# A decoder layer with a mixture of experts on one core: the experts' first layer as seven block products of half-sized matrices in place of eight, and the cross-attention's normalisation moved from VectorE to GpSimd

## The reference

```python
x = layernorm(x + self_attention(x))            # 16 heads of 16, rotary positions
x = layernorm(x + cross_attention(x, context))  # masked keys, biases
# mixture of 8 experts, 2 per token, capacity 1280 tokens each
h = gelu(einsum("ecd,edh->ech", buf, w1) + b1, approximate=False)   # 256 -> 1024
out = einsum("ech,ehd->ecd", h, w2) + b2                            # 1024 -> 256
x = layernorm(x + sum over the token's two experts of gate * out)
```

## Time and profile before

| | |
|---|---|
| median of 3 runs | 2143.32 us (2142.54 to 2143.4) |
| the profiled execution, its own time | 2142.94 us |
| its span, first to last instruction | 2140.8 us |
| attentions, busy: PE, DVE, POOL | 1469.0, 1160.5, 689.4 of 1548.4 us |
| experts, busy: PE, DVE, ACT, POOL | 573.3, 141.3, 155.1, 150.8 of 592.4 us |
| mean granted clock of TensorE | 0.98 |

### The profile page before, as it was taken

How to read it: one execution, slowest core, us unless ns; L and a number is a source line. 1 busy time by engine, 2 the same in 40 slices (tenths; PEclk the granted TensorE clock), 3 DMA queues, 4 the chain that set the end, 5 groups by cost and what they waited for, 6 DMA issues and landing times. The chain is left out here.

```text
span 2140.8 us, 55059 instructions
## 1 busy us (share of the span) xinstructions
PE 2042.3 (95%) x21891; PEld 1516.0 (71%) x21891; DVE 1301.8 (61%) x2740; ACT 989.1 (46%) x1515; POOL 840.1 (39%) x1134
## 2 busy tenths in 40 slices
PE   7899999999999999999999999988699999999996
PEld 4667777777776777777777767766478787878785
DVE  5678778788778787787887787865211111111146
ACT  1455555555555555555555555544231212121233
POOL 3333454544444444545445444432412121212144
PEclk8899999999999999999999999998899999999998
DMA  3331112111011111000111100100123323332363
GB/s 97 98 114 51 43 40 82 36 58 43 28 39 30 30 34 38 29 28 26 31 35 28 32 26 25 31 21 19 53 50 87 72 33 84 87 72 33 84 228 148
DMA packets 99531, 118.80 MB, mean 55 GB/s; under 512 B 12144, under 2 KB 92221, under 8 KB 97232
## 3 DMA queue, kind: packets, MB, share of 16 engines
q1 hardware_dynamic: 69856, 83.75, 12.4%
q0 software_dynamic: 17184, 19.66, 5.2%
q10 hardware_dynamic: 12240, 11.88, 1.6%
HBM read 66.11 MB, written 56.12 MB: 57 GB/s over the span
## 5 line engine op out<-in xcount | busy, mean ns | idle before, releaser
L992 DVE TENSOR_REDUCE smax<-ps_s 128x4 f32<-128x1024 f32 x508 | 619.2, 1219 | 209.4 <-PE ps_s L661 197.4
L868 ACT ACTIVATE prob<-ps_e 128x1024 f32<-128x1024 f32 x508 | 519.7, 1023 | 466.5 <-PE ps_e L674 327.0
L1833 ACT ACTIVATE hid<-m_ps_h,b_sb 128x320 f32<-128x320 f32 x256 | 134.7, 527 | 392.4 <-PE m_ps_h L1787 392.4
L661 PE MATMUL ps_s<-stack_kh,stack_q 32*128 32x256 f32 x2032 | 305.3, 307 | 0.8 <-ACT stack_q L857 0.8
L674 PE MATMUL ps_e<-stack_q,stack_kh 32*128 32x256 f32 x2032 | 293.7, 281 | 0.0
L1787 PE MATMUL m_ps_h<-m_cols,w_sb 128*128 128x320 f32 x1024 | 292.4, 435 | 0.6 <-DVE m_cols L1856 0.6
L674 PE MATMUL ps_e<-stack_q,stack_kl 32*128 32x256 f32 x2032 | 289.9, 277 | 0.0
L1804 PE MATMUL m_ps_o<-w_sb,hid 128*128 128x256 f32 x1280 | 279.2, 380 | 1.4 <-DVE m_res L1885 1.4
L661 PE MATMUL ps_s<-stack_kl,stack_q 32*128 32x256 f32 x2032 | 276.6, 278 | 0.0
L1804 PEld LDWEIGHTS m_ps_o<-w_sb,hid 128*128 128x128 f32 x1280 | 243.7, 190 | 35.9 <-DVE m_res L1885 1.8
L1676 POOL DMA_INDIRECT sums_dram<-m_res,m_token x70 | 108.2, 1546 | 399.7 <-DVE m_res L1920 346.5
(11 more groups left out here) (169 smaller groups left out, 3665.0 us busy)
## 6 DMA issues: line engine op xcount, KB each, us to landing
w_sb<-in_w SPq DMA_DIRECT2D x16, 1024.0 KB, 7.5
slot_rows_dram<-w_sb ACTq DMA_DIRECT2D x40, 258.0 KB, 2.8
m_rows<-slot_rows_dram SPq DMA_DIRECT2D x15, 645.0 KB, 4.8
xT<-in_xT SPq DMA_DIRECT2D x32, 256.0 KB, 3.0
ctxT<-in_ctxT SPq DMA_DIRECT2D x32, 256.0 KB, 2.8
x_res<-in_x SPq DMA_DIRECT2D x32, 256.0 KB, 2.8
sums_dram<-x SPq DMA_DIRECT2D x32, 256.0 KB
c_rows<-sums_dram SPq DMA_DIRECT2D x8, 1024.0 KB, 15.5
```

What stands on the lines that cost most here:

```text
L661: return nc.tensor.matmul(out, stack_q[at_side][rows, g, t * P:(t + 1) * P], (stack_kh, stack_kl)[part][at_side][rows, g, :], start=(X == ...
L868: nc.scalar.activation(prob[:, h:h + 2, :].rearrange("p h s -> p (h s)"), shifted[:, :, :, :].rearrange("p h t s -> p (h t s)"), ACT.Exp, ...
L992: nc.vector.tensor_reduce(max_columns(X, p), scores[:, :, :, :], AX.X, ALU.max)\
L1833: nc.scalar.activation(hid[:, m, half * HALF:(half + 1) * HALF], ps_h[:, (2 * m + half) % 4, 0:HALF], ACT.Gelu, bias=b1_sb[:, pe_, m:m + 1 ...
```

## The change

For chunks 1 to 13 (`SEVEN`), the 256x1024 weights and the 256x640 columns are taken as 2x2 blocks (input feature halves by halves of the hidden features; by halves of the tokens), and the product of two 2x2 matrices of blocks is formed with seven block products and sums. A block product has 4 pieces of 128 hidden features (`PAIRS`, index i), each one 128x128 by 128x320 matmul without accumulation: 28 matmuls a chunk. The sums around them: GpSimd makes four sums of weight blocks per expert (128x512) and four of column blocks per chunk (128x320); per i, ScalarE copies the products P1 and P2 out of PSUM, VectorE makes six sums (three of which are the results C22, C12, C21 before gelu), GpSimd the seventh (C11), and ScalarE applies gelu from SBUF in place. The transposes and the notes of the next chunk move from `hidden` into and behind `output`. Chunks 0, 14 and 15 stay as they were. In the attentions `second_normed` moves from VectorE's queue at k = 1 to GpSimd's, right behind `inverse_deviation`, one half step earlier in the order written out.

The diff, cut (`STORED_FIRST` is 2 of the 5 tiles; headings between @@ say where the lines stand):

```diff
@@ attentions: VectorE's part, then GpSimd's @@
-            def second_normed(b):
...
-                normalise(CROSS, b, y2, x2)
-                    if is_of(CROSS, q) and k == 1:
-                        second_normed(q[1])
+            def second_normed(b):
...
+                pool.wait_ge(ln_r[CROSS].sem, ln_r[CROSS].count(b))
+                ready()
+                for t in range(T2):
+                    nc.gpsimd.tensor_scalar(x2[:, t, :], y2[:, t, :], mv[CROSS][:, t, 0:1], rstd[CROSS][:, t:t + 1],
+                                            ALU.subtract, ALU.mult).then_inc(ln[CROSS].sem, 1)
                 if is_of(CROSS, p):
                     inverse_deviation(CROSS, p[1])
+                    second_normed(p[1])
@@ experts, GpSimd @@
+        def weight_sums(e):
...
+            nc.gpsimd.tensor_tensor(w_sums[:, 0, :], halves[1][0], halves[1][1], ALU.add).then_inc(w_made.sem, 1)
...
+        def column_sums(q, u):
+            halves = [[cols[:, u, k, half * HALF:(half + 1) * HALF] for half in range(2)] for k in range(KD)]
+            pool.wait_ge(t_ev.sem, t_ev.count(q))
+            nc.gpsimd.tensor_tensor(c_sums[:, 0, :], halves[0][1], halves[0][0], ALU.subtract).then_inc(c_made.sem, 1)
+            nc.gpsimd.tensor_tensor(c_sums[:, 2, :], halves[1][1], halves[0][1], ALU.subtract).then_inc(c_made.sem, 1)
+            pool.wait_ge(c_made.sem, c_made.count(at, 1))
+            nc.gpsimd.tensor_tensor(c_sums[:, 1, :], halves[1][1], c_sums[:, 0, :], ALU.subtract).then_inc(c_made.sem, 1)
+            pool.wait_ge(c_made.sem, c_made.count(at, 3))
+            nc.gpsimd.tensor_tensor(c_sums[:, 3, :], halves[1][0], c_sums[:, 1, :], ALU.subtract).then_inc(c_made.sem, 1)
+        def first_sums(q):
+            pool.wait_ge(o_mm.sem, o_mm.count(q - 1))
+            for i in range(PAIRS):
+                pool.wait_ge(p_ev.sem, p_ev.count(turn_of(q), 2 * i + 2))
+                nc.gpsimd.tensor_tensor(hid[:, i, 0:HALF], p1_part[:, i % 2, :], p2_part[:, i % 2, :], ALU.add)\
+                  .then_inc(sum11.sem, 1)
         for q in range(LAST):
-            store(q, q // per_expert, q % 2, 0)
+            stored = 0
+            if q in SEVEN:
+                first_sums(q)
+            if q + 1 in SEVEN:
+                pool.wait_ge(h_mm.sem, h_mm.count(q))
+                if q + 1 == SEVEN[0] or (q + 1) % per_expert == 0:
+                    weight_sums((q + 1) // per_expert)
+                wait_for_rows(q)
+                store(q, q % 2, 0, STORED_FIRST)
+                stored = STORED_FIRST
+                column_sums(q + 1, (q + 1) % 2)
+            else:
+                wait_for_rows(q)
+            store(q, q % 2, stored, CT)
@@ experts, TensorE @@
+        def hidden_by_seven(q, u, pe_, e):
...
+            for i in range(PAIRS):
+                if i > 0:
+                    pe.wait_ge(summed.sem, sum_of(q, i - 1, SUM22))
+                part(P1, i, w[0][0], x[0][0])
+                if i == 0:
+                    pe.wait_ge(c_made.sem, c_made.count(turn_of(q)))
+                else:
+                    pe.wait_ge(p_ev.sem, p_ev.count(turn_of(q), 2 * i))
+                part(P6, i, s[1], t[1])
+                if i > 0:
+                    pe.wait_ge(summed.sem, sum_of(q, i - 1, SUM12))
+                part(P5, i, s[0], t[0])
+                if i > 0:
+                    pe.wait_ge(summed.sem, sum_of(q, i - 1, SUM21))
+                part(P7, i, s[2], t[2])
+                pe.wait_ge(p_ev.sem, p_ev.count(turn_of(q), 2 * i + 1))
+                part(P2, i, w[0][1], x[1][0])
+                pe.wait_ge(summed.sem, sum_of(q, i, U2))
+                part(P3, i, s[3], x[1][1])
+                pe.wait_ge(summed.sem, sum_of(q, i, U4))
+                part(P4, i, w[1][1], t[3])
@@ experts, TensorE, output(q): the blocks of hid in the order 0 4 1 5 2 6 3 7, and @@
+                if q in SEVEN:
+                    for n in COLUMNS_BEHIND[c]:        # ((0, 1), (2, 3), (4,), (), ())
+                        to_columns(q + 1, (q + 1) % 2, n)
@@ experts, ScalarE @@
+            def last_two(i):
+                act.wait_ge(summed.sem, sum_of(q, i, SUM21))
+                gelu(PAIRS + i, 0)
+                act.wait_ge(sum11.sem, sum11.count(turn_of(q), i + 1))
+                gelu(i, 0)
+            for i in range(PAIRS):
+                copied(P1, i, p1_part)
+                if i > 0:
+                    last_two(i - 1)
+                copied(P2, i, p2_part)
+                act.wait_ge(summed.sem, sum_of(q, i, SUM22))
+                gelu(PAIRS + i, 1)
+                act.wait_ge(summed.sem, sum_of(q, i, SUM12))
+                gelu(i, 1)
+            last_two(PAIRS - 1)
@@ experts, VectorE, per i; one() waits for the product, then adds PSUM and SBUF, 128x320 @@
+                dve.wait_ge(p_ev.sem, p_ev.count(turn_of(q), 2 * i + 1))
+                one(P6, i, u2_part[:, :], p1_part[:, i % 2, :])
+                dve.wait_ge(summed.sem, sum_of(q, i, U2))
+                one(P5, i, u4_part[:, :], u2_part[:, :])
+                one(P7, i, u3_part[:, :], u2_part[:, :])
+                dve.wait_ge(summed.sem, sum_of(q, i, U4))
+                one(P7, i, hid[:, PAIRS + i, HALF:CHUNK], u4_part[:, :])
+                one(P3, i, hid[:, i, HALF:CHUNK], u4_part[:, :])
+                dve.wait_ge(summed.sem, sum_of(q, i, U3))
+                one(P4, i, hid[:, PAIRS + i, 0:HALF], u3_part[:, :])
```

More of the change, by code:

```diff
@@ L94, in due, with __init__, count @@
         return not isinstance(value, int) or value > 0
+class Varied:
+    def __init__(self, sem, sizes):
+        self.sem, self.sizes = sem, sizes
+        self.before = [0] + list(itertools.accumulate(sizes))
+    def count(self, b, k=None):
+        return self.before[b] + (self.sizes[b] if k is None else k)
+    def due(self, b):
+        return b >= 0
 class Drams:
@@ L1572, in run_experts @@
     t_ev = Steps(sem("m_t_ev"), CT)
-    h_mm = Steps(sem("m_h_mm"), 2 * FT)
+    LAST = CHUNKS - per_expert
+    SEVEN = range(1, LAST)
+    PAIRS = FT // 2
+    P1, P6, P5, P7, P2, P3, P4 = range(1, 8)
+    C22, C12, C21, C11 = range(1, 5)
+    U2, U4, U3, SUM22, SUM12, SUM21 = range(1, 7)
+    PRODUCTS, SUMS, OUTPUTS = 7, 6, 4
+    COLUMNS_BEHIND = ((0, 1), (2, 3), (4,), (), ())
+    STORED_FIRST = 2
+    w_sums = sb("w_sums", [P, 4, F // 2])
+    c_sums = sb("c_sums", [P, 4, HALF])
+    p1_part = sb("p1_part", [P, 2, HALF])
+    p2_part = sb("p2_part", [P, 2, HALF])
+    u2_part = sb("u2_part", [P, HALF])
+    u3_part = sb("u3_part", [P, HALF])
+    u4_part = sb("u4_part", [P, HALF])
+    w_made = Steps(sem("m_w_made"), 4)
+    c_made = Steps(sem("m_c_made"), 4)
+    p_ev = Steps(sem("m_p_ev"), 2 * PAIRS)
+    sum11 = Steps(sem("m_sum11"), PAIRS)
+    summed = Steps(sem("m_summed"), SUMS * PAIRS)
+    h_mm = Varied(sem("m_h_mm"), [PRODUCTS * PAIRS if q in SEVEN else 2 * FT for q in range(CHUNKS)])
     h_ev = Steps(sem("m_h_ev"), 2 * FT)
@@ L1615, in run_experts, with turn_of, product, at_bank @@
     block = ctx.enter_context(nc.Block())
+    def turn_of(q):
+        return q - SEVEN[0]
+    def product(q, i, k):
+        return h_mm.count(q, PRODUCTS * i + k)
+    def at_bank(i, k):
+        return ps_h[:, (PRODUCTS * i + k - 1) % 4, 0:HALF]
+    def sum_of(q, i, k):
+        return summed.count(turn_of(q), SUMS * i + k)
     def rows_in_count(q, u):
@@ L1672, in store @@
                 pool.wait_ge(sent.sems[1], sent.count(q - 1, 1))
-            for c in range(CT):
+        def store(q, u, first, end):
+            for c in range(first, end):
                 pool.wait_ge(o_done.sem, o_done.count(q, c + 1))
@@ L1792, in hidden, with part @@
                     to_columns(q + 1, 1 - u, m - 2)
+        def hidden_by_seven(q, u, pe_, e):
+            w = [[w1_sb[pe_][:, k, m * (F // 2):(m + 1) * (F // 2)] for k in range(KD)] for m in range(2)]
+            x = [[cols[:, u, k, half * HALF:(half + 1) * HALF] for half in range(2)] for k in range(KD)]
+            s, t = [w_sums[:, n, :] for n in range(4)], [c_sums[:, n, :] for n in range(4)]
+            if u == 0:
+                pe.wait_ge(w_in.sems[pe_], w_in.count(e, pe_))
+            pe.wait_ge(w_made.sem, w_made.count(e))
+            pe.wait_ge(t_ev.sem, t_ev.count(q))
+            pe.wait_ge(h_ev.sem, h_ev.count(q - 1))
+            def part(k, i, left, right):
+                nc.tensor.matmul(at_bank(i, k), left[:, i * P:(i + 1) * P], right, start=True, stop=True)\
+                  .then_inc(h_mm.sem, 1)
+            for i in range(PAIRS):
[19 more added lines that the diff above has]
+                part(P4, i, w[1][1], t[3])
         def output(q, pe_):
@@ L1821, in normalise, with gelu_by_seven, gelu, copied @@
                                  scale=rstd[:, q, g:g + 1]).then_inc(by_act.sem, 1)
+        def gelu_by_seven(q, pe_):
+            def gelu(m, half):
+                rows = hid[:, m, half * HALF:(half + 1) * HALF]
```

(35 more changed lines are left out.)

54 lines of the change are left out of this document (41 added, 13 removed).

## The result

Median 2168.93 us (2166.65 to 2170.93, 4 runs) against 2142.93 us of before (4 runs): ratio 1.0121, 95% interval 1.0104 to 1.0139. Slower by 26 us, where 18 us faster was forecast.

The account below looks back on a forecast made before the run. TensorE was taken to bound the kernel, by matmuls in the experts and a ring with VectorE in the attentions; -28.0 + 7.3 + 2.0 = -18.7 us against 2142.94 gave 2124.2, predicted as 2124.5, range 2112 to 2138 us.

Parts of the forecast that it names:

- The seven products: Experts, TensorE: 4 of 32 matmuls of 320 columns removed in each of 13 chunks, 28.0 us gained.
- three covers: Experts: conditions for the 28.0 us: the loop over i closes, GpSimd's sums are in time, the border to `output` is hidden.
- The price of the moved instruction: Attentions, GpSimd: each of two normalising instructions of 128x256 costs 0.90 us, between 0.42 and 1.56.
- Forecast A: The prediction's main case: 2121 to 2130 us by the bounds of its terms; chance 46%.
- y's lateness: Attentions: GpSimd's queue is late by 1.98 us, less 1.59 us idle, so its y comes 0.39 us late.
- The 0.25 us per half step: Attentions: duo 4 late by 0.25 us (0.18 to 0.39) in 29 half steps, +7.3 us (5.2 to 11.3).
- VectorE's relief: Attentions: `second_normed` leaving VectorE frees 1.37 us there in the half step shown, but gives TensorE nothing by itself.
- The attentions' end: Nothing hides the moved normalisation before TensorE's transposes of x2 and GpSimd's scatters: +2.0 us (1.0 to 3.3).
- D: Attentions: the GpSimd instruction costs 1.56 us, duo 4 waits 1.5 to 1.7 us 29 times: 2164 us; chance 9%.
- C: Experts: the loop over i doesn't close, P1 waits some 0.25 us 52 times, 13 us: 2137 us; chance 13%.
- B: Attentions: GpSimd's normalisation costs 0.70 us or less each, y is not late: 2116 us; chance 24%.
- E: Attentions: VectorE's relief reaches TensorE, the 0.48 us idle before duo 4 go 29 times, 14 us: 2102 us; chance 8%.

## Why the prediction was wrong, point by point

- **The seven products: right.** 28.0 us forecast; 13 x (35.60 - 33.44) = 28.1 in the trace, 28.7 as a run by itself. Its three covers held: between 1642 and 2077 us TensorE has no idle time before any product of `hidden`. VectorE's sums took 0.488 us (0.49 said), ScalarE's gelus from SBUF 0.559 (0.53 to 0.65), its copies 0.426 (at most 0.53).
- **The price of the moved instruction: the step that failed.** "I take it as near to L1287 itself, 0.90 us": it measured 1.22 us (1.36 where only one was there). With two operations it lies between the 0.90 of one and the upper bound of 1.56. Forecast A held this price fixed: its range moved only the lag of duo 4 and the end, though the price was the least known of its terms. The gap before it was 0.34 us, not 0.18, so GpSimd was late by 0.34 + 2.43 = 2.8 us in place of 1.98.
- **y's lateness.** 0.39 us forecast, 1.11 measured. The way that it takes was right: GpSimd's idle time of 1.59 us, then y, the statistics, `smax`, duo 4. The runs with half the instructions, with `place` behind and with useless copies showed it. The 0.25 us per half step, meant to lie between 0.18 and 0.39, came as 1.11, as the lag after `smax` stayed 0.22 us. That the trace calls the wait "issue" I read as a proof that something other than VectorE held duo 4; the kernel before with two lines of VectorE's queue moved showed the contrary. That VectorE's relief gives TensorE nothing came true for another reason: freed of the normalisation, VectorE waits 0.94 us for TensorE's scores before its next reduction (at 584.52 us in the changed kernel's trace), where it didn't wait before.
- **TensorE's clock: left out.** No term had it. The longer waits bring the clock to its lower level in 13 turns, which is 16 to 21 us. Without it the change would have cost some 10 us (the run with the filled waits).
- **The attentions' end.** +2.0 forecast. From the `rstd` start to TensorE's transposes of x2 it is 1575.98 - 1572.38 = 3.60 us where it was 1522.76 - 1521.11 = 1.65, 1.95 more; the whole end, from the last steady turn to the experts' first matmul, is 6 us longer, of which the rest wasn't followed up: its cause stays open.
- **The rivals.** It went as D, the case on the other side, at its turning point: with 1.22 us it "decides from about 1.2 us on", and 29 waits of 1.1 us would be 32 us, just more than the 28 won (the trace has 26 such turns, 29 us). What made it 26 us slower and not a few is the clock and the end. C (the loop doesn't close) and B were wrong. E was right in that 14 us lay before duo 4 for the taking, and wrong in the way: an order of two lines had to move, not VectorE's load.

In sum, in us: -28.7 for the products; +29.1 for the waits (the 27 steady turns of the run with the filled waits, 1251.3, less the 1222.2 of before); +16 to 21 for the clock; +6 for the end. The last three make 51 to 56, against the 54.5 of the normalisation alone. With the measured price, its own terms would have given -28 + 26 to 34 + 2, between no change and 8 us of loss; the rest of the miss is the clock, which no term had, and the end.

## What to carry to other kernels

An operation that goes to an engine "with time to spare" costs what it makes late, not what it takes: measure the idle time just ahead of the next result that others wait for in that queue (here 1.59 us), and compare it with the upper bound of the new work, not with the nearest row. When a wait on TensorE's path grows, put a price on the clock too (here 16 to 21 us beside 29 of waiting). And look what stands ahead of the critical operation in its own queue: here two lines that put the statistics behind the reduction were worth more than half of what the arithmetic saved, and made the lateness harmless.

## What the runs showed of the hardware that wasn't expected

- GpSimd's tensor_scalar with two operations and two operands per partition takes 1219 ns for 128x256 f32, and 1360 ns in the run where VectorE's half of the same work (421 ns) ran beside it; a cast of twice the elements takes 610. In that run the one of the 32 instructions on GpSimd that VectorE's half didn't overlap took 1227, and in two others GpSimd's took 1223 and 1224 and VectorE's half 616 and 646. So work side by side slows GpSimd too, by 0.14 us; before only VectorE's side of it was seen (1.37 against 0.73 us).
- TensorE's idle time of 1.59 us once in a turn of 46 us, where 0.48 had been, brings stretches at 1.2 GHz in half of the turns; filled to 0.50 us with work whose results nobody reads, it brings none.
- An idle time of TensorE whose end the trace calls "issue" can still be a wait for another engine: duo 4 started 0.21 to 0.22 us after VectorE's reduction in both kernels, while duo 3 ahead of it, which TensorE reached without idle time, started 0.06 us after the reduction before it (757.39 against 756.12 + 1.21 in the kernel before).
